# Routing work of a hybrid transformer kernel dealt over more attention steps, with square roots moved to GpSimd

## What is computed

```python
x = x + attn_a(layernorm(x))      # 16 heads of 8, causal softmax
x = x + ffn(layernorm(x))
x = x + attn_b(layernorm(x))      # 16 heads of 8, distance softmax, no mask
x = x + ffn(layernorm(x))

def ffn(flat_x):                  # 4096 tokens, 8 experts, 2 per token
    logits = flat_x @ Wr
    top_vals, top_idx = top_k(logits, 2)
    rw = softmax(top_vals)
    combine = sum(rw[..., None] * one_hot(top_idx, 8), axis=1)
    h = silu(flat_x @ Wg[e]) * (flat_x @ Wu[e])          # 128 -> 512
    eo = (h @ Wd[e]) * 12 ** -0.5                         # 512 -> 128
    out = sum over e of combine[:, e] * eo[:, e]
```

## Time and profile before

| | us |
|---|---|
| median of three runs | 1128.7 |
| lowest and highest | 1120.68 and 1128.79 |
| the profiled execution's own time | 1131.86 |
| its span | 1130.1 |
| mean granted TensorE clock over the span | 0.934 |

### The profile page before, as it was taken

How to read it: one execution, slowest core, us unless ns; L and a number is a source line. 1 busy time by engine, 2 the same in 40 slices (tenths; PEclk the granted TensorE clock), 3 DMA queues, 4 the chain that set the end, 5 groups by cost and what they waited for, 6 DMA issues and landing times.

```text
span 1130.1 us, 28620 instructions
## 1 busy us (share of the span) xinstructions
PE 1007.8 (89%) x9290; PEld 713.5 (63%) x9290; DVE 758.6 (67%) x2285; ACT 676.6 (60%) x1399; POOL 535.9 (47%) x756
## 2 busy tenths in 40 slices
PE   2999999998989999999797989999989899999990
PEld 1455555554578999999443434444444789999990
DVE  4688888777775333456778889999867663334443
ACT  2377777755644545556286878998848445555550
POOL 3244446635724600545886554556807336005565
PEclk9999999988989999999688989999968799999995
DMA  5445656434147978887643323434311469788873
GB/s 151 112 113 131 146 146 172 134 87 91 51 146 213 272 225 250 255 257 228 153 98 77 98 68 86 100 94 87 88 29 54 152 198 284 230 235 275 270 223 114
DMA packets 201721, 175.02 MB, mean 155 GB/s; under 512 B 19812, under 2 KB 160616, under 8 KB 201576
## 3 DMA queue, kind: packets, MB, share of 16 engines
q1 hardware_dynamic: 193384, 156.41, 49.8%
q0 software_dynamic: 8192, 16.79, 5.1%
HBM read 122.99 MB, written 50.14 MB: 153 GB/s over the span
## 4 chain that ended last, share of the span: by engine, by line
PE 66%; DVE 15%; issue 6%; DMA 6%; SPq 3%; POOL 3%; ACT 1%; POOLq 0%; DVEq 0%; ACTq 0%
PE psS L1384 10%; PE psT L1391 10%; PE psS L356 9%; PE psO L322 7%; DVE mx L662 5%; PE psO L1407 5%; PE psN L1407 5%; PE psS L387 4%; PE psM L277 3%; PE psT L364 2%; PE psN L329 2%; PE psM L427 2%; DMA wuc<-in_L_ffn_Wu 1%; POOL xg L1267 1%; PE psM L1372 1%
## 5 line engine op out<-in xcount | busy, mean ns | idle before, releaser
L662 DVE TENSOR_REDUCE mx<-psS 128x3 f32<-128x384 f32 (+1 forms) x512 | 309.2, 617 | 87.4 <-PE psS L387 47.4
L356 PE MATMUL psS<-kst,qst 48*128 48x256 bf16 (+1 forms) x1024 | 196.2, 280 | 43.0 <-DVE mx L662 31.6
L559 ACT ACTIVATE pT<-psT,scb 128x512 f32<-128x512 f32 x256 | 193.3, 772 | 52.7 <-PE psT L364 50.2
L1448 DVE TENSOR_TENSOR hT<-sg,psT 128x512 f32<-128x512 f32 x142 | 97.5, 686 | 159.8 <-PE psT L1391 131.6
L364 PE MATMUL psT<-qst,kst 50*128 50x256 bf16 (+1 forms) x1024 | 191.4, 273 | 4.6 <-DMA qst<-scr_m 2.1
L1267 POOL DMA_INDIRECT xg<-xn,slot x128 | 123.2, 963 | 135.5 <-DVE ysb L1443 72.8
L1384 PE MATMUL psS<-xTt,wgc 128*128 128x128 f32 x1136 | 153.6, 279 | 4.7 <-issue 4.5
L554 ACT ACTIVATE pT<-psT 128x384 f32<-128x384 f32 x256 | 123.3, 488 | 52.4 <-PE psT L364 44.0
L1391 PE MATMUL psT<-xTt,wuc 128*128 128x128 f32 x1136 | 152.5, 278 | 2.2 <-DMA wuc<-in_L_ffn_Wu 2.1
L356 PEld LDWEIGHTS psS<-kst,qst 48*128 48x128 bf16 x1024 | 63.0, 96 | 142.8 <-DVE mx L662 75.6
L1384 PEld LDWEIGHTS psS<-xTt,wgc 128*128 128x128 f32 x1136 | 140.5, 195 | 7.4 <-issue 7.0
(11 more groups left out here) (227 smaller groups left out, 1607.1 us busy)
## 6 DMA issues: line engine op xcount, KB each, us to landing
wgc<-in_L_ffn_Wg SPq DMA_DIRECT2D x142, 256.0 KB
wuc<-in_L_ffn_Wu SPq DMA_DIRECT2D x142, 256.0 KB
scr_part<-part SPq DMA_DIRECT2D x128, 128.0 KB, 2.2
qst<-scr_part SPq DMA_DIRECT2D x64, 192.0 KB, 3.5
kst<-scr_part SPq DMA_DIRECT2D x64, 192.0 KB, 4.5
xin<-xg SPq DMA_DIRECT2D x142, 64.0 KB
eo<-ysb SPq DMA_DIRECT2D x142, 64.0 KB
scr_part<-part SPq DMA_DIRECT2D x32, 192.0 KB, 2.0
```

Of the source, the lines that this page charges most:

```text
L356: return nc.tensor.matmul(ps[:, c0:c0 + n], q_[r64, t, q0], k_[r64, t, 0:n], start=(half == 0), stop=True, skip_group_check=True)
L559: nc.scalar.activation(pT[:, g % 8, 0:cols], psT[g % 2][:, 0:cols], ACT.Exp, scale=scb[r][:, 0, i:i + 1], bias=scb[r][:, 1, i:i + 1]).then ...
L662: nc.vector.tensor_reduce(mx3[:, u, 0:n, pos:pos + 1].rearrange("p a b -> p (a b)"), psS[h % 2][:, 0:kcols(L)].rearrange("p (a k) -> p a k ...
L1448: nc.vector.tensor_tensor(out=hT[(n0 + k) % FETCH][:].rearrange("p a c -> p (a c)"), in0=sg[p][:], in1=psT[p][:], op=ALU.mult).then_inc(f[ ...
```

## The change

Nothing that is computed changes, other than how an inverse root is computed. Six edits:

1. The second layer's four roots (blocks 16 to 23 in step 6, 24 to 31 in step 9, 0 to 7 in step 11, 8 to 15 in step 12) are computed by POOL as `(var + eps) ** -0.5`: an add and a power on a 128x8 tile (`pool_root`), behind `pool_split` and the gathers of the step. DVE keeps statistics and `bn_aggr` (`dve_moments`). The tile `half` of exponents grows from one row to 128.
2. Statistics of blocks 0 to 15 move from steps 11 to 13 into steps 10 to 12.
3. POOL's normed tokens: 4 blocks in step 11, 6 in 12, 6 in 13 (before: 8 in 14, 8 in 15).
4. Transposes: two quads in step 13 and two in step 14, behind heads 4 and 8, through the bank `psO[1]` (before: heads 2 to 5 of step 16, through `psM`). Logits: one quad behind each of heads 3 to 6 of step 15. Picks at heads 7, 8, 10, 11 of step 15. Counts behind head 2 of step 16 and the five slot parts at heads 4, 6, 8, 10, 12.
5. Scatters: 2 in step 16, 16 in step 17, 14 in step 18.
6. The first layer's logits: one quad behind each of heads 3 to 6 of step 14 (before: two behind head 3, two behind head 4); its first and third pick parts two heads and one head later.

```diff
+        def dve_moments(lo, hi):
+            for k in range(lo, hi):
+                ins = nc.vector.bn_aggr(mean_rstd[:, k, :], bn6[:, k, :])
+            ins.then_inc(s_moments, 1)
+
+        def pool_root(pool, lo, hi, moments, done):
+
+            pool.wait_ge(s_moments, moments)
+            v, rstd = nwt[:, 0, lo:hi], mean_rstd[:, lo:hi, 1]
+            nc.gpsimd.tensor_scalar(v, rstd, EPS, None, ALU.add).then_inc(s_var, 1)
+            pool.wait_ge(s_var, moments)
+            nc.gpsimd.tensor_tensor(out=rstd, in0=v, in1=half[:, 0:hi - lo], op=ALU.pow).then_inc(done, 1)
...
-            return psO[1] if n % G == 1 and i == QUADS[1] - 1 else psM
+            return psO[1] if n == 2 or n % G == 1 and i == QUADS[1] - 1 else psM
...
+        ROUTE_AT = {4: 4, 6: 5, 8: 5.5, 10: 6, 12: 7}
+        THIRD_TOKENS = {11: (0, 4), 12: (4, 10), 13: (10, SIZE[0])}
+        SCATTER_AT = {16: H, 17: 0, 18: 0}
+        THIRD_SCATTERS = {16: (0, 2), 17: (2, 18), 18: (18, 32)}
...
+                if l == 1 and j in (6, 9) and h == H:
+                    lo = SIZE[0] + 8 * (j // 9)
+                    pool_root(pool, lo, lo + 8, 1 + j // 9, s_lnB)
+                if l == 1 and j in (11, 12) and h == H:
+                    lo = SIZE[0] // 2 * (j - 11)
+                    pool_root(pool, lo, lo + SIZE[0] // 2, j - 8, s_ln[2])
+                if l == 1 and j in THIRD_TOKENS and h == H:
+                    pool.wait_ge(s_ln[2], 1 if j == 11 else 2)
+                    for k in range(*THIRD_TOKENS[j]):
...
+                if l == 1 and j in (16, 17, 18) and h == SCATTER_AT[j]:
+                    for i in range(*THIRD_SCATTERS[j]):
+                        if j > 16:
+                            pool.wait_ge(s["exp"], 16 * (j - 3) + i - THIRD_SCATTERS[j][0] + 1)
+                        pool_scatter(pool, 2, i)
...
-                if l == 0 and j == 14 and h in (3, 4):
+                if l == 0 and j == 14 and 3 <= h < 7:
                     if h == 3:
                         pe.wait_ge(L.s["oT"], 2 * (j - 4) + 2)
-                    for i in range(2 * (h - 3), 2 * (h - 3) + 2):
-                        pe_logits(pe, 0, i)
+                    pe_logits(pe, 0, h - 3)
...
+                if l == 1 and j in (13, 14):
+                    if h == 4:
+                        pe.wait_ge(L.s["oT"], 2 * (j - 4) + 2)
+                    if h in (4, 8):
+                        pe_tokens(pe, n, 2 * (j - 13) + h // 8)
+                    if h == 12:
+                        pe.wait_ge(r_sem["T"], quads(n) + 2 * (j - 12))
+                if l == 1 and j == 15:
+                    if h == 3:
+                        pe.wait_ge(L.s["oT"], 2 * (j - 4) + 2)
+                    if 3 <= h < 7:
+                        pe_logits(pe, n, h - 3)
+                    if h == 12:
+                        pe.wait_ge(r_sem["lg"], LG_COPIES[n] + 1)
+                if l == 1 and j == 16 and h == 2:
+                    pe.wait_ge(L.s["bc"], 2 * (B - 1))
+                    pe_counts(pe, n)
+                if l == 1 and j == 16 and h == 8:
+                    pe.wait_ge(r_sem["cnt"], n + 1)
...
+        def dve_third_route(dve, j, h):
+
+            n, size = 2, SIZE[0]
+            if (j, h) == (15, 7):
+                dve_logits(dve, n, 0, QUADS[0], LG_COPIES[n] + 1)
+                dve_pick_top(0, 0, size)
+            if (j, h) == (15, 8):
+                dve_pick_mark(0, 0, size)
+            if (j, h) == (15, 10):
+                dve_pick_top(1, 0, size)
+            if (j, h) == (15, 11):
+                dve_pick_mark(1, 0, size)
+                dve_picked(dve, n)
+            if (j, h) == (16, 3):
+                dve_counts(dve, n)
+            if j == 16 and h in ROUTE_AT:
+                dve_route_part(dve, n, ROUTE_AT[h])
```

More of the change, by code:

```diff
@@ L126, in build @@
         prow = sb("prow", [1, 5, H])
-        half = sb("half", [1, H])
+        half = sb("half", [P, H])
         scb = [sb(f"scb{r}", [P, 2, H]) for r in range(RING)]
@@ L198, in build @@
         s_half = sem("s_half")
+        s_moments = sem("s_moments")
+        s_var = sem("s_var")
         s_lnB = sem("s_lnB")
@@ L727, in pool_chain @@
             done(1)
-            nc.gpsimd.tensor_tensor(out=S2, in0=V, in1=half[:], op=ALU.pow).then_inc(s["pool"], 1)
+            nc.gpsimd.tensor_tensor(out=S2, in0=V, in1=half[0:1, :], op=ALU.pow).then_inc(s["pool"], 1)
             done(3)
@@ L1645, in hook @@
                     act_weights(act, 0)
-                if l == 1 and j == 16 and 3 <= h < 7:
-                    act_tokens(act, 2, h - 3)
-                if l == 1 and j == 16 and h == 11:
+                if l == 1 and j in (13, 14) and h in (5, 9):
+                    act_tokens(act, 2, 2 * (j - 13) + h // 8)
+                if l == 1 and j == 15 and h == 13:
                     act_weights(act, 2)
@@ L1764, in dve_second_half @@
             if (j, h) == (9, 5):
-                dve_aggr(mid, hi)
-                dve_root_begin(mid, hi)
-            if (j, h) == (9, 9):
-                dve_root_refine(mid, hi)
-            if (j, h) == (10, 5):
-                dve_root_refine(mid, hi)
+                dve_moments(mid, hi)
             if (j, h) == (10, 9):
-                dve_root_end(mid, hi, s_lnB)
                 dve.wait_ge(s_lnB, 4)
         def dve_third_group(dve, j, h):
-            hi = SIZE[0]
-            if j in (11, 12) and h == 9:
+            mid, hi = SIZE[0] // 2, SIZE[0]
+            if (j, h) in ((10, 5), (11, 5), (12, 5)):
                 dve.wait_ge(LB.s["x1"], 2 * (j - 4))
+            if (j, h) == (10, 5):
+                dve_stats(0, 4)
+            if (j, h) == (10, 9):
+                link(dve_stats(4, mid))
+            if (j, h) == (11, 5):
+                dve_moments(0, mid)
+                dve_stats(mid, mid + 2)
             if (j, h) == (11, 9):
-                dve_stats(0, 4)
+                dve_stats(mid + 2, hi - 2)
             if (j, h) == (12, 5):
-                dve_stats(4, 8)
+                link(dve_stats(hi - 2, hi))
             if (j, h) == (12, 9):
-                dve_stats(8, 12)
-            if (j, h) == (13, 5):
-                link(dve_stats(12, hi))
-            if (j, h) == (13, 9):
-                dve_aggr(0, hi)
-            if (j, h) == (14, 5):
-                dve_root_begin(0, hi)
-                dve_root_refine(0, hi)
-            if (j, h) == (14, 9):
-                dve_root_refine(0, hi)
-                dve_root_end(0, hi, s_ln[2])
+                dve_moments(mid, hi)
+        def dve_third_route(dve, j, h):
[14 more added lines that the diff above has]
+                dve_route_part(dve, n, ROUTE_AT[h])
         def dve_beside(l):
@@ L1823, in hook @@
                     dve_first_route(dve, j, h)
[L1824 to L1833 removed]
+                if l == 1 and j in (15, 16):
+                    dve_third_route(dve, j, h)
                 if j == 18 and h == 15:
```

42 lines of the change are left out of this document (3 added, 39 removed).

## The result

The changed kernel takes 1118.57 us (median of four runs, 1111.73 to 1122.49) against 1128.74 us; the ratio is 0.9893 with a 95% interval of 0.9853 to 0.9934. In a second comparison, with six runs, it was 0.9869 (0.9834 to 0.9904). Forecast were 1114 us and a range of 1104 to 1133; the time lies inside, and the change is faster by a little over 1%. The profiled execution took 1122.49 us with a span of 1120.4, which is 3.9 above its median, as the one before was 3.2 above its own.

What follows compares the result with a forecast made beforehand. The prediction took PE, ACT and DVE in lockstep as the bound, with second-layer step 16 17.7 us over. Terms from -12.0 (step 16) to +8.0 (step 15) summed to -14.4 us: 1128.7 to 1114, range 1104 to 1133.

Steps and rivals of the forecast that it cites:

- The bound: Second-layer quiet steps: PE, ACT and DVE in lockstep at 16.7 us, DVE with some 2 us to spare.
- Roots off DVE: Second-layer steps 6, 7 and 9: root instructions stretched by POOL's split leave DVE, saving 5.3 us.
- The power on POOL: Inverse roots on POOL: a 128x8 power costs 1.5 us, priced by columns, and stays hidden.
- slow-power rival: POOL's power is slow and delays PE; hidden up to 4.3 us, at 17 us the kernel takes 1140; chance 12%.
- Step 14 and the transposes: Second layer: step 14 loses 2.6 us (root 3.5 less, transpose quads 0.9 more); transposes add 0.7 in step 13.
- Step 15: Second layer: gains logits and picks, some stretched by POOL's split; +8.0 us, bounds 5 and 11, to 24.7.
- Step 16: Second layer: keeps only counts and slot parts besides attention, clock near 1.00; -12.0 us, to 20.0.
- The scatters: Two scatters go early, at the end of step 16, so POOL's end comes 2.5 us earlier; PE must follow.
- The sum: All terms over the changed steps together: -14.4 us, giving 1114.
- clock rival: Low PE clock through half of steps 15 and 16, step 17's gain not won; 1124 us, chance 22%.

Runs made afterwards that it cites:

- the experiment with three powers: Changed kernel with two extra powers into a spare tile in each of the four roots; ratio 0.9892.
- the kernel with both moves: Changed kernel with step 15's picks behind POOL's split and expert-output additions of steps 4 and 5 behind head 12; 1106.98 us, ratio 0.9786; again 1108.43 us, 0.9802.

## Why the prediction was right

**The bound** was read rightly: three engines in lockstep, with DVE's 2 us to spare deciding what is free. The quiet steps stayed at 16.7 while roots left and statistics came.

**Roots off DVE** were sized at 5.3 us in steps 6, 7 and 9 and brought 5.2 there, and 1.9 more in steps 8 and 10, which the sum had at nothing. The experiment with them alone gives 7.2 or 5.4 by the windows and 7.0 by the ratio. The mechanism (a root instruction waits for POOL's split) is the one that the picks and the additions show again; that a one-input instruction of the root waits too was not seen. The 1.4 of step 8 is luck: its clock had been 0.91, and over all profiles it is either 18.1 or 19.5, with the old roots as with the new.

**The power on POOL** was taken at 1.5 us and is 1.68, to the side that was chosen. The slow-power rival (12%) falls, and by the experiment with three powers its threshold was too low.

**Step 14 and the transposes** came at -2.7 and +0.5 against -2.6 and +0.7. That -2.7 is so near is in part luck as well: the step before stood at clock 0.92, and at 1.00 it takes 18.8 with the root in it.

**Step 15** was the term most off: +9.8 against +8.0, inside its bounds of 5 and 11. Two stretched picks were counted, at 1.1 us together, although twice the 0.7 of its own rows is 1.4; two came, 0.9 each. The picks were read as 4.9 us, but in the rows of before, less the maximum and the addition to `x` between them, they are 4.3. These two slips nearly cancel. The sum gave DVE's excess 4.0 us of the step's length, and PE's waits came to 3.3. What was not counted is the low level, which began in PE's wait behind the picks: PE was busy 23.21 us, where the 16.2 of a quiet step and 4.0 of logits had been counted. The experiment that moved the picks took 4.1 us off the step in three of four profiles and nothing in the fourth.

**Step 16** came at -12.5 against -12.0, though at clock 0.82 and not near 1.00: DVE, not PE, was its bound. **The scatters** came at -2.9 against -2.5 in the profile; no timing shows them. No run takes steps 14 to 16 apart from the rest of the change. By the ratios the whole change gains 5 to 8 us beyond the roots of steps 6 and 9, with intervals that touch; how this divides over transposes, picks, slots and scatters is read from the windows alone.

**The sum** of the changed steps was -15.7 against -14.4, and the measured change by the medians is -10.2 and by the two ratios -12.1 and -14.8. The first profile had 6 us against it in untouched stretches, and one 3.2 us piece of these was gone in the second. So the forecast of 1114 is right in most of its parts, 4.6 us too low for the first comparison and level with the second; that the parts sum so closely owes something to step 8 and to step 14. The clock rival (22%) came in part: the clock falls in step 15, though not in step 16 for as long as before, and the gain of the scatters' place was there in the profile. It was priced as a case that happens or doesn't. The runs show it as a thing that one and the same code does in some executions, for 5.9 us in step 15 and 4.4 in first-layer step 14.

**What the clock decided.** In two profiles of the changed kernel the low level began within PE's wait of 2.86 us. In one execution of the kernel with both moves it began between the first two quads of logits, with PE waiting for nothing over 0.3 us there, and in another it did not. The Trainium skill, TensorE: Matmul & The Clock Gate, Part 1 on the HAM clock gate, says that idleness brings the low level back. The first case agrees with it. The second it does not tell apart from its twin, and no run here does.

## What to carry to other kernels

Look up, for each DVE instruction with two SBUF inputs, what POOL does at its time: beside a two-input elementwise POOL instruction on 128x512 it took 1.2 us in place of 0.3, and a one-input TENSOR_SCALAR there took 0.89 in place of 0.17. Moving sixteen such instructions three heads later, one line, took 8.5 us off two steps, and the ratio from 0.987 to 0.980: about half of what the whole change was worth. Before dealing work out over steps, ask whether it leaves the full engine or only moves on it; here the gain was in what left DVE (roots), in waits that went, and hardly in how logits were spread. And take two profiles of each kernel before explaining a step, whether the change touches it or not: step 8 had its two lengths with the old code as with the new.

## What the runs showed that was not expected

POOL's power does not hold DVE up as its split does: eight two-input additions beside a 1x16 power in step 7 took 0.33 to 0.35 us each, before and after the change, and beside the split 1.2 to 1.3. There it was the power that got longer, 4.06 us in place of 2.92 in the changed kernel. And identical code had a step of 22.4 or 28.3 us by the granted clock alone (0.95 or 0.70), with nothing in the rows ahead of it to tell the two executions apart.
